# The head of a graph network's kernel, rearranged: one load queue in order of need, uneven chunks, a one-operation order check

## What is computed

```python
def sage(x, src, dst, Wl, bl, Wr):
    agg = segment_max(x[src], dst)               # -inf for a node without edges
    agg = where(isfinite(agg), agg, 0.0)
    return agg @ Wl + bl + x @ Wr

h = maximum(layernorm(x), 0.0)                   # 6250 x 128: "h0"
h = leaky_relu(sage(h, src, dst, Wl1, bl1, Wr1)) # 128 -> 256
h = leaky_relu(sage(h, src, dst, Wl2, bl2, Wr2)) # 256 -> 256
h = leaky_relu(sage(h, src, dst, Wl3, bl3, Wr3)) # 256 -> 128
return x + h
```

## Time and profile before

| what | before |
|---|---|
| median of 3 timed runs | 6193.24 us (6192.94 to 6194.87) |
| the profiled execution's own time | 6178.24 us |
| its span in the trace | 6176.4 us |
| POOL busy | 4607.9 us, 75% of the span |
| DVE busy | 2882.1 us, 47% |
| PE busy | 695.5 us, 11% |
| ACT busy | 227.9 us, 4% |
| gathers at L365 | 4692, mean 946 ns |

### The profile page before, as it was taken

How to read it: one execution, slowest core, us unless ns; L and a number is a source line. 1 busy time by engine, 2 the same in 40 slices (tenths; PEclk the granted TensorE clock), 3 DMA queues, 4 the chain that set the end, 5 groups by cost and what they waited for, 6 DMA issues and landing times. The chain is left out here.

```text
span 6176.4 us, 24426 instructions
## 1 busy us (share of the span) xinstructions
PE 695.5 (11%) x2214; PEld 399.1 (6%) x2214; DVE 2882.1 (47%) x3614; ACT 227.9 (4%) x664; POOL 4607.9 (75%) x4878
## 2 busy tenths in 40 slices
PE   0111111111100780000000000057000000000003
PEld 0000000000000340000000000034000000000002
DVE  4333333333333555555555555565555555555556
ACT  1000000000000110000000000011000000000001
POOL 6777777777777677777777777767777777777776
PEclk8555555555555655555555555565555555555556
DMA  4333333333333576666666666667666666666665
GB/s 129 107 107 108 105 107 107 107 107 107 107 104 107 171 236 210 209 210 209 210 211 210 211 209 210 209 205 246 210 210 210 210 211 208 212 208 210 209 210 171
DMA packets 435669, 1088.94 MB, mean 176 GB/s; under 512 B 101413, under 2 KB 154154, under 8 KB 435642
## 3 DMA queue, kind: packets, MB, share of 16 engines
q0 software_dynamic: 206976, 530.17, 30.4%
q1 hardware_dynamic: 203706, 537.55, 23.4%
q10 hardware_dynamic: 24960, 20.95, 1.1%
HBM read 555.13 MB, written 533.14 MB: 176 GB/s over the span
## 5 line engine op out<-in xcount | busy, mean ns | idle before, releaser
L365 POOL DMA_INDIRECT ring<-features,stage x4692 | 4439.4, 946 | 1451.3 <-issue 1406.8
L656 DVE TENSOR_TENSOR ring<-banks,ring 128x1024 f32<-128x1024 f32 (+1 forms) x1173 | 1226.5, 1046 | 3066.8 <-DMA ring<-features,stage 3049.3
L635 DVE TENSOR_TENSOR banks<-ring,banks 128x1024 f32<-128x1024 f32 (+1 forms) x1173 | 1232.2, 1050 | 37.6
L869 PE MATMUL banks<-ident,ring 128*128 128x128 f32 x20 | 5.0, 428 | 3763.5 <-DVEq L668 3763.5
L843 PE MATMUL banks<-dst_low,own 128*128 128x394 bf16 x200 | 99.5, 498 | 1459.8 <-DVE own L619 1459.8
L869 PEld LDWEIGHTS banks<-ident,ring 128*128 128x128 f32 x20 | 3.9, 222 | 3764.9 <-DVEq L668 3538.1
L827 PE MATMUL banks<-wr,h_turned 128*128 128x256 f32 (+1 forms) x490 | 204.0, 559 | 95.9 <-ACT h_turned L965 95.9
L1009 ACT ACTIVATE agg<-zeros 128x512 f32<-128x512 f32 x75 | 47.3, 630 | 3957.4 <-PE banks L901 3957.4
L390 POOL DMA_INDIRECT ring<-running_max_log,end_row x147 | 141.6, 964 | 60.5 <-issue 43.9
L624 DVE COPY stage<-edges 128x8 int32 (+1 forms) x588 | 129.1, 220 | 84.8 <-DVE banks L635 25.8
L829 PE MATMUL banks<-b,ones 1*128 1x256 f32 (+1 forms) x294 | 141.9, 579 | 0.0
(11 more groups left out here) (104 smaller groups left out, 560.8 us busy)
## 6 DMA issues: line engine op xcount, KB each, us to landing
running_max_log<-ring SPq DMA_DIRECT2D x782, 512.0 KB, 3.2
running_max_log<-ring SPq DMA_DIRECT2D x391, 256.0 KB, 2.3
ring<-features,stage POOLq DMA_INDIRECT x4692, 2.8
h_in<-features ACTq DMA_DIRECT2D x98, 128.0 KB
features<-h_out SPq DMA_DIRECT2D x48, 256.0 KB, 2.2
ring<-x SPq DMA_DIRECT2D x5, 640.0 KB, 10.4
features<-ring SPq DMA_DIRECT2D x5, 640.0 KB, 3.7
h_in<-features ACTq DMA_DIRECT2D x49, 64.0 KB
```

The lines of the kernel that those rows point to most:

```text
L365: pool.indirect_dma_start(ring[:, c * w:(c + 1) * w], None, tables[l], bass.IndirectOffsetOnAxis(ap=stage[:, b, u:u + 1].bitcast(U32), axi ...
L635: dve.tensor_tensor(sum_ps[:, 0:CHAINS * w].rearrange("p (h f) -> p h f", h=CHAINS), group(g - 1).rearrange("p (h f) -> p h f", h=CHAINS), ...
L656: dve.tensor_tensor(group(g), sum_ps[:, 0:CHAINS * w], group(g), ALU.max).then_inc(turn, 1)
```

## The change

- **Loads.** SP issues all loads of the head, in the order x0, x1, x2, dst, x3, x4, src. ACT issues none. dst comes with a word more on either side of each run (393 words instead of 391), in one transfer with overlapping sources, so the eight transfers of single words go. `prev_last` and `next_first` become views of it. The weights are loaded behind the last store of h0.
- **Chunks.** x goes in chunks of 6, 11, 12, 12 and 8 tiles; the padding tile is left out. ACT normalises 4, 8, 9, 8 and 3 of them, POOL 2, 3, 3, 4 and 2, and DVE itself the last 3 tiles.
- **Order of DVE.** `normalise` of a chunk moves into the statistics of the next one, behind four bn_stats. The order check moves behind all statistics. It becomes one `tensor_tensor_reduce` (subtract, then the maximum along the row) over int32 dst, and one small comparison.
- **`stage`.** It is filled straight from src before the branch; the reordering of src comes behind the branch.
- **`prep`.** Its scratch moves from `restart` to `own`, and the restart terms are made from the differences of the order check in one operation where two stood.
- **ACT.** A one-element square root (`warm`) stands ahead of all else on ACT, and with it the loading of its table.

```diff
-TAIL_TILES = 10
 STORES = 5
-ACT_TILES = 7
+CHUNKS = (6, 11, 12, 12, 8)
+ACT_TILES = (4, 8, 9, 8, 3)
+POOL_TILES = (2, 3, 3, 4, 2)
+VARS_AFTER = (4, 8, 6, 3)
+RECIPROCAL_AFTER = 4
...
+    dst_seen = bass.AP(dst.tensor, 0, [[RUN, P], [P * RUN, CHAINS], [1, RUN + 2]])
...
-        dst_t = own[:, 6 * BANK:6 * BANK + COLS].bitcast(I32)
+        dst_w = own[:, 6 * BANK:6 * BANK + COLS + 2 * CHAINS].bitcast(I32).rearrange("p (h j) -> p h j", h=CHAINS)
+        falls = own[:, 10 * BANK:10 * BANK + COLS].rearrange("p (h j) -> p h j", h=CHAINS)
+        scratch = own[:, 14 * BANK:14 * BANK + COLS].rearrange("p (h j) -> p h j", h=CHAINS)
...
+        dst_runs = dst_w[:, :, 1:RUN + 1]
+        prev_last, next_first = dst_w[:, :, 0], dst_w[:, :, RUN + 1]
...
-            for s in range(TAIL_STEPS):
-                share = slice(s * TAIL_TILES + ACT_TILES, (s + 1) * TAIL_TILES)
+            for s in range(HEAD_STEPS):
+                share = slice(FROM[s] + ACT_TILES[s], FROM[s] + ACT_TILES[s] + POOL_TILES[s])
                 pool.wait_ge(norm_ready, 2 * (s + 1))
                 for k in range(share.start, share.stop):
                     pool.tensor_scalar(h0_all[:, k, :], x_all[:, k, :], rstd[:, k:k + 1], shift[:, k:k + 1],
                                        ALU.mult, ALU.add).then_inc(h0_scaled, 1)
-                pool.wait_ge(h0_scaled, (TAIL_TILES - ACT_TILES) * (s + 1))
+                pool.wait_ge(h0_scaled, sum(POOL_TILES[:s + 1]))
...
                 dve.wait_ge(x_loaded[s], DMA)
                 if s:
-                    dve.wait_ge(var_done, TAIL_TILES * s)
-                for k in range(TAIL_TILES):
-                    dve.bn_stats(stats[:, k, :], x_all[:, s * TAIL_TILES + k, :]).then_inc(stats_done, 1)
-                dve.wait_ge(stats_done, TAIL_TILES * (s + 1))
-                for k in range(TAIL_TILES):
-                    dve.bn_aggr(mean_var[:, s * TAIL_TILES + k, :], stats[:, k, :]).then_inc(var_done, 1)
+                    dve.wait_ge(var_done, FROM[s])
+                for k in range(CHUNKS[s]):
+                    if s and k == RECIPROCAL_AFTER:
+                        normalise(s - 1)
+                    dve.bn_stats(stats[:, k, :], x_all[:, FROM[s] + k, :]).then_inc(stats_done, 1)
+                dve.wait_ge(stats_done, FROM[s + 1])
+                for k in range(CHUNKS[s]):
+                    dve.bn_aggr(mean_var[:, FROM[s] + k, :], stats[:, k, :]).then_inc(var_done, 1)
 
             def normalise(s):
 
 
-                t = slice(s * TAIL_TILES, (s + 1) * TAIL_TILES)
+                t = slice(FROM[s], FROM[s + 1])
                 dve.wait_ge(std_done, s + 1)
                 dve.reciprocal(rstd[:, t], std[:, t]).then_inc(norm_ready, 1)
                 dve.wait_ge(norm_ready, 2 * s + 1)
                 dve.scalar_tensor_tensor(out=shift[:, t], in0=mean_var[:, t, 0], scalar=-1.0,
                                          in1=rstd[:, t], op0=ALU.mult, op1=ALU.mult).then_inc(norm_ready, 1)
 
-            scratch_runs = restart.rearrange("p (h j) -> p h j", h=CHAINS)
-
-            def check_order():
-
-                dve.wait_ge(order_loaded, (LOADS - 1) * DMA)
-                dve.tensor_tensor(scratch_runs[:, :, 1:RUN], dst_runs[:, :, 1:RUN], dst_runs[:, :, 0:RUN - 1],
-                                  ALU.is_lt).then_inc(order_checked, 1)
-                dve.tensor_tensor(scratch_runs[:, :, 0], dst_runs[:, :, 0], prev_last[:, :],
-                                  ALU.is_lt).then_inc(order_checked, 1)
-                dve.wait_ge(order_checked, 2)
-                dve.tensor_reduce(disorder[:, :], restart[:, :], AXIS.X, ALU.add).then_inc(order_checked, 1)
-
-            for s in range(TAIL_STEPS):
+            for s in range(HEAD_STEPS):
                 statistics(s)
-                if s == 0:
-                    check_order()
-                else:
-                    normalise(s - 1)
-            normalise(TAIL_STEPS - 1)
+            normalise(HEAD_STEPS - 1)
+
+            rest = slice(FROM[HEAD_STEPS - 1] + ACT_TILES[-1] + POOL_TILES[-1], END_TILES)
+            dve.wait_ge(norm_ready, 2 * HEAD_STEPS)
+            for k in range(rest.start, rest.stop):
+                dve.tensor_scalar(h0_all[:, k, :], x_all[:, k, :], rstd[:, k:k + 1], shift[:, k:k + 1],
+                                  ALU.mult, ALU.add).then_inc(h0_last_scaled, 1)
+            dve.wait_ge(h0_last_scaled, rest.stop - rest.start)
+            dve.tensor_scalar(h0_all[:, rest, :], h0_all[:, rest, :], 0.0, None, ALU.max).then_inc(h0_last_done, 1)
+
+            dve.wait_ge(dst_loaded, DMA)
+            dve.tensor_tensor_reduce(out=falls, in0=dst_w[:, :, 0:RUN], in1=dst_runs, scale=1.0, scalar=0.0,
+                                     op0=ALU.subtract, op1=ALU.max, accum_out=highest_fall[:, :]
+                                     ).then_inc(order_checked, 1)
+            dve.wait_ge(order_checked, 1)
+            dve.tensor_scalar(disorder[:, :], highest_fall[:, :], 0.0, None, ALU.is_gt).then_inc(order_checked, 1)
+
+            def stage_first():
+
+                dve.tensor_copy(stage[:, 0:BLOCKS - 1, :].rearrange("p b (j h) -> p (b j) h", h=CHAINS),
+                                src_runs.rearrange("p (h j) -> p j h", h=CHAINS)[:, 0:(BLOCKS - 1) * BLOCK_GROUPS, :]
+                                ).then_inc(first_staged, 1)
+
+            dve.wait_ge(src_loaded, DMA)
+            stage_first()
...
+            dve.wait_ge(first_staged, 1)
+            dve.sem_inc(block_scanned, BLOCKS - 1)
             dve.tensor_copy(src_turns, src_runs.rearrange("p (h j) -> p h j", h=CHAINS)).then_inc(prep_done, 1)
-            dve.wait_ge(prep_done, 1)
-            dve.tensor_copy(stage[:, 0:BLOCKS - 1, :],
-                            src_t[:, 0:(BLOCKS - 1) * BLOCK_COLS].rearrange("p (b u) -> p b u", u=BLOCK_COLS)
-                            ).then_inc(block_scanned, BLOCKS - 1)
-
-            scratch = restart[:, :].bitcast(I32)
-            scratch_ints = scratch.rearrange("p (h j) -> p h j", h=CHAINS)
-            dve.tensor_scalar(scratch, dst_t, P - 1, None, ALU.bitwise_and).then_inc(prep_done, 1)
+            dve.tensor_scalar(scratch_ints, dst_runs, P - 1, None, ALU.bitwise_and).then_inc(prep_done, 1)
...
-            dve.tensor_tensor(restart_turns[:, :, 1:RUN], dst_runs[:, :, 1:RUN], dst_runs[:, :, 0:RUN - 1],
-                              ALU.not_equal).then_inc(prep_done, 1)
+            dve.tensor_scalar(restart_turns[:, :, 1:RUN], falls[:, :, 1:RUN], 0.0, LOWEST,
+                              ALU.not_equal, ALU.mult).then_inc(prep_done, 1)
...
-            act.dma_start(dst_runs, dst.rearrange("(h p) j -> p h j", p=P)).then_inc(order_loaded, DMA)
-            act.wait_ge(const_done, 2)
-            with nc.allow_non_contiguous_dma(reason="one word of each run of edges"):
-                for dest, there in run_neighbours(dst):
-                    act.dma_start(dest, there).then_inc(order_loaded, DMA)
-            act.dma_start(src_runs.rearrange("p (h j) -> p h j", h=CHAINS),
-                          src.rearrange("(h p) j -> p h j", p=P)).then_inc(src_loaded, DMA)
-
             def deviation(s):
 
-                t = slice(s * TAIL_TILES, (s + 1) * TAIL_TILES)
-                act.wait_ge(var_done, TAIL_TILES * (s + 1))
+                t = slice(FROM[s], FROM[s + 1])
+                act.wait_ge(var_done, FROM[s + 1])
                 nc.scalar.activation(std[:, t], mean_var[:, t, 1], ACT.Sqrt, bias=eps[:, 0:1]).then_inc(std_done, 1)
 
+            act.wait_ge(const_done, 1)
+            nc.scalar.activation(warm[:, :], eps[:, :], ACT.Sqrt).then_inc(act_ready, 1)
+            act.wait_ge(act_ready, 1)
+            deviation(0)
+            for s in range(HEAD_STEPS):
+                act.wait_ge(norm_ready, 2 * (s + 1))
+                for k in range(ACT_TILES[s]):
+                    if s < HEAD_STEPS - 1 and k == VARS_AFTER[s]:
+                        deviation(s + 1)
+                    t = FROM[s] + k
+                    nc.scalar.activation(h0_all[:, t, :], x_all[:, t, :], ACT.Relu, bias=shift[:, t:t + 1],
+                                         scale=rstd[:, t:t + 1]).then_inc(h0_done, 1)
+                if s < HEAD_STEPS - 1 and VARS_AFTER[s] == ACT_TILES[s]:
+                    deviation(s + 1)
...
-            for s in range(TAIL_STEPS):
-                t = slice(s * TAIL_TILES, (s + 1) * TAIL_TILES)
+            def load_x(s):
+
+                t = slice(FROM[s], FROM[s + 1])
                 sp.dma_start(x_all[:, t, :], x_rows[:, t, :]).then_inc(x_loaded[s], DMA)
+
+            for s in range(3):
+                load_x(s)
+            sp.dma_start(dst_w, dst_seen).then_inc(dst_loaded, DMA)
+            for s in range(3, HEAD_STEPS):
+                load_x(s)
+            sp.dma_start(src_runs.rearrange("p (h j) -> p h j", h=CHAINS),
+                         src.rearrange("(h p) j -> p h j", p=P)).then_inc(src_loaded, DMA)
```

(7 more changed lines are left out.)

96 lines of the change are left out of this document (44 added, 52 removed).

## The result

| | before | after |
|---|---|---|
| median of 10 runs | 6193.21 us (6192.24 to 6194.87) | 6176.91 us (6166.68 to 6178.44) |
| the profiled execution | 6178.24 us | 6166.68 us |
| its first gather starts at | 46.03 us | 31.87 us |
| its 57th gather starts at | 119.73 us | 104.13 us |

The changed kernel is 16.3 us faster, a ratio of 0.9972 with a 95% interval from 0.9963 to 0.9981. The forecast was 6178.0 us, 15.2 us faster, in a range of 6174.5 to 6182.3. The total came out as forecast, but two terms of its sum did not, as the head shows. The lowest of the ten, 6166.68, is the profiled execution; the other nine lie between 6174.66 and 6178.44.

What follows compares the result with a forecast made beforehand. A string of 4692 gathers at about 1.25 us bounds the kernel, with the head added one for one. First gather 16.2 us earlier less 1.0 lost gives 15.2 us, from 6193.2 to 6178.0 us; range 6174.5 to 6182.3.

Steps and rivals of the forecast that it cites:

- What held the head before: Head of the old kernel: DVE stood still 7.99 us for the single words of `next_first`, a late small transfer.
- Transfers: New head: loads and stores on one queue without a gap, last store landed at 29.4 us, plus 0.4 us delay.
- The check of 1.78 us: DVE's order check behind all statistics: one operation priced as L452, 1.78 us, ending at 23.8 us.
- The rival of twice its length: Order check on DVE takes 3.6 us; first gather at 30.7 us, median 6178.9 us; chance 0.10.
- The branch on POOL is as long, and its cover is the wait for the last store.: Head, POOL: its branch takes as long as DVE's, which ends at 27.0 us, hidden under the wait for the store.
- The loss of the gathers: Behind the first gather: DVE's `prep` costs the gathers 4.5 us (3.8 to 5.0), 1.0 us more than before.
- 80% of the length: First gathers: they lose 80% of the large DVE operations' length, as 4.4 us of L571 and L575 cost 3.5.
- Its own signs: Head and gathers: store-released start 29.4 to 30.9, check 1.8, DMA full 2 to 29, ten gathers 15 to 17 us, 946 ns elsewhere.
- Contention: POOL's last share and first gathers lose all of DVE's large operations; start 30.9, loss 6.2, median 6180.8 us; chance 0.18.
- The faster transfers: Head loads so fast that arithmetic alone bounds; first gather at 27.4 us, median 6175.6 us; chance 0.10.
- the slower rival: All 4692 gathers: buffers move, each gather takes 5.9 ns more, 27.6 us in all; 6205.6 us; chance 0.03.
- The 15 us between the profiled and the timed runs: Whole run: timed runs lie 15.0 us above the profiled execution, taken as the same for both kernels.

Runs made afterwards that it cites:

- before_check_late: The kernel before with only its order check moved behind the last normalise; first gather at 37.41 us, median 8.6 us below before, ratio 0.9986.
- check_in_two: The changed kernel with the order check as two operations, a subtraction and a maximum; first gather at 33.63 us, median 15.9 us below before, ratio 0.9974.
- prep_late: The changed kernel with DVE's prep held back until the first block's gathers have landed; first gather at 31.93 us, median 14.9 us below before, ratio 0.9976.
- weights_late: The changed kernel with the weight loads held back until the first block's gathers have landed; first gather at 31.60 us, median 17.0 us below before, ratio 0.9972.
- check_early: The changed kernel with the order check between chunks 3 and 4's statistics and POOL out of the last chunk; median 18.8 us below before, ratio 0.9969.

## Why the prediction came out right, and where it was wrong

- **What bounds the kernel: right.** A string of gathers that did not change, and a head that is added one for one. Start and first gathers give 15.6 us, the medians 16.3.
- **What held the head before: right.** DVE's stand for the late single words was the cause by before_check_late, 8.6 us.
- **Transfers: right.** x0 at 4.26 (forecast 4.0), x1 at 6.77 (6.5), x3 at 14.46 (14.1), last store landed at 29.90 against 29.8. But the last agrees by luck: the bound was not the queue, which had holes from 23 to 29 us, but POOL's last share, done at 26.40 where 23.9 stood in the sum. Of these 2.5 us 0.7 are an earlier delay (its share of chunk 3 began at 19.57, not 18.9) and 1.8 DVE's effect on the last share, for which the forecast gave 0 to 2.9. The loads were a little faster, 303 GB/s instead of 285, which took up part.
- **The check of 1.78 us: right, 1.77.** The rival of twice its length is not seen. Nor is the half rate of the Trainium skill (Vector Engine (DVE) Microarchitecture Reference, section 7), by which the forecast put this operation on two int32 sources in SBUF at 3.6 us: it takes what L452 takes in the earlier trace rows. The page states the rule for one instruction form, S2S2D2_STT, and the profile calls this operation CUSTOM_DVE_ANT_1; no run shows whether the rule was meant for it. check_in_two shows that a second operation would have cost its whole length.
- **The step that failed: "The branch on POOL is as long, and its cover is the wait for the last store."** The branch was priced by DVE's: 2.19 us between the copy and the next operation in the sum, 1.70 measured. DVE's was over at 27.97 (27.0 in the sum, since the check ended at 25.2 and not 23.8) and cost nothing. Behind POOL's, by the traces, instructions have to be fetched, and the fetch stood behind the stores until 29.79. With 2.08 us behind it the start is 31.87 and not 29.8. Taking the branch away brings 1.6 us at the start and 1.8 in the median. In the kernel before, the fetch at 42.20 allowed a gather from about 42.20 + 2.05 = 44.25, 1.8 us ahead of the 46.03 that the store set, so nothing in its timeline pointed at it.
- **The loss of the gathers, mis-sized: forecast 4.5, measured 2.3.** POOL started 2.1 us late, and half of `prep` was over by then. With all of it beside gathers (prep_late) the loss is 4.1, inside the forecast's 3.8 to 5.0. But "80% of the length" was not the mechanism. The four short operations (L581) and the reduction (L584) held nothing, and most long gathers end 0.11 to 0.12 us behind a DVE operation over the whole array with one input: the 2.38 us (34.25) behind L577 (34.14), the two in prep_late, and the gather of 4.28 us behind L575 in the earlier trace rows, 53.01 and 52.89. The one of 1.79 us doesn't fit as well: it ends at 40.09, 0.69 us behind L591. No run puts each kind of operation beside gathers by itself. The gathers that end with the DVE operation agree with the lock in the Trainium skill (SBUF — State Buffer, section "SBUF: two separate sides"), which the page ties to DVE's two-port modes and to its operations with two inputs in SBUF. In which mode an operation ran the trace doesn't show.
- **The sum: right because the two errors cancel.** 2.1 us late at the start, 2.2 to 2.4 less lost behind it. The total was right by luck.
- **Its own signs: three of five failed.** The first gather came at 31.87, outside 29.4 to 30.9, and "issue" released it, not the store. The transfers had holes (share 0.76 and 0.80 from 23 to 29 us), and the forecast had called such a hole a sign that it was wrong. The first ten gathers took 13.5 us and not 15 to 17. The check of 1.8 us and the gathers of 946 ns came as stated.
- **The rivals.** Contention came out in part: POOL's last share lost 1.8 of the 2.9 us, the gathers 2.3 of 6.2. The faster transfers were not the bound. The gather's period stayed at 0.946 + 0.30, so the slower rival did not come.
- **The 15 us between the profiled and the timed runs, "for a reason the trace doesn't show".** Most of it is likely in the gathers. Some executions have a mean of 949 ns instead of 946 for all 4692 of them, as the profiled one of weights_late:

```profile
span 6178.1 us, 24413 instructions
L377 POOL DMA_INDIRECT ring<-features,stage x4692 | 4451.1, 949 | 1454.7 <-issue 1401.0
```

That is 12.7 us more of busy time than in the changed kernel's row above, at the same idle time, and the medians of before, 6193 and 6196 us in two series and 6183 in two others, lie apart by 10 to 13. What sets it stays open. The kernel before has no trace at this level, so for its own 15 us this is an inference from the other kernels.

Two points are open. The medians gain 0.4 to 2.2 us more than the 57th gather shows in every kernel, and check_early gains most of all. All kernels share the one trace of before, and its execution (6178.24) is 2.9 us below the lowest of the 48 timed ones at 6183, so a part may lie in that baseline; no run here tells. And that the fetch waits for the stores is read from its place behind them (27.14 to 29.79, against 1.1 us on idle engines in the kernel before and in check_early); no run put a known load in its way.

## What to carry to other kernels

Look in the head of a kernel for a small late transfer on which a busy engine stands in the middle of its work; moving the step that needs it brought 8.6 of the 14.2 us at the start. Loads that are needed first should not share the DMA engines with those that can wait (5.0 us). Transfers ahead of an engine's arithmetic hold its whole stream until the last is issued. Before a branch on a value is put close to the end of a chain, count what lies behind it on each engine: here POOL, by the traces, had to fetch instructions, and an old cover of 1.8 us had hidden that.
